# A mixture-of-experts block: six tiles of surplus blocks taken out of the mixed stage and put ahead of the one-expert tiles

## The reference

```python
x = x + jnp.tanh(g_xattn[0]) * _L0_xattn_ref(_layernorm(x, axis=-1), ctx_1024, L0_xattn_W, L0_xattn_b)
x = x + jnp.tanh(g_ffn[0]) * _L0_ffn_ref(_layernorm(x, axis=-1), L0_ffn_expert_sel, L0_ffn_keys, L0_ffn_values)
# _L0_ffn_ref, with xf the 2048 x 256 tokens:
logits = xf @ expert_sel.T
sel = jax.nn.sigmoid(logits)
sel_val, sel_idx = jax.lax.top_k(sel, N_HEADS)          # N_HEADS = 4
gates = gates.at[jnp.arange(N)[:, None], sel_idx].set(sel_val)
h = jnp.einsum('nd,kde->nke', xf, keys)                 # keys 64 x 256 x 128
scores = jax.nn.relu(h) * gates[:, :, None]
out = jnp.einsum('nke,kev->nv', scores, values)         # values 64 x 128 x 256
```

## Time and profile before

| | us |
|---|---|
| median of three runs | 301.71 (300.08 to 302.07) |
| the profiled execution's own time | 301.05 |
| its span, first to last instruction | 299.3 |
| PE / DVE / ACT / POOL busy | 209.5 / 131.7 / 108.9 / 139.1 |

### The profile page before, as it was taken

How to read it: one execution, slowest core, us unless ns; L and a number is a source line. 1 busy time by engine, 2 the same in 40 slices (tenths; PEclk the granted TensorE clock), 3 DMA queues, 4 the chain that set the end, 5 groups by cost and what they waited for, 6 DMA issues and landing times. The chain is left out here.

```text
span 299.3 us, 4532 instructions
## 1 busy us (share of the span) xinstructions
PE 209.5 (70%) x1316; PEld 155.0 (52%) x1316; DVE 131.7 (44%) x496; ACT 108.9 (36%) x307; POOL 139.1 (46%) x156
## 2 busy tenths in 40 slices
PE   7998677549576713398866786939596987613874
PEld 6765545337344401277755575727465665303653
DVE  4478576554754726211221111523251533253674
ACT  3587566637544620033433243413131434200100
POOL 3006745746574766315655665635363655640000
PEclk9999959968755555579999999977686999855998
DMA  5999999999999692377954554533442431129996
GB/s 147 294 307 333 310 353 361 363 344 338 330 288 316 184 320 79 92 206 216 360 183 129 168 148 138 171 93 99 127 134 76 141 103 49 52 69 352 397 414 240
DMA packets 40895, 66.03 MB, mean 221 GB/s; under 512 B 5381, under 2 KB 24603, under 8 KB 40864
## 3 DMA queue, kind: packets, MB, share of 16 engines
q1 hardware_dynamic: 32572, 46.68, 50.0%
q0 software_dynamic: 6624, 16.82, 16.1%
q10 hardware_dynamic: 1668, 2.17, 2.0%
HBM read 38.31 MB, written 28.64 MB: 224 GB/s over the span
## 5 line engine op out<-in xcount | busy, mean ns | idle before, releaser
L525 POOL DMA_INDIRECT y_rows<-rows,by_place x74 | 72.8, 983 | 69.7 <-ACT rows L1042 52.8
L515 POOL DMA_INDIRECT x_slots<-rows,pos_i x64 | 63.5, 992 | 56.4 <-DVE pos_i L1115 33.4
L1293 DVE TENSOR_SCALAR shared<-bank 128x256 f32<-128x256 f32 (+1 forms) x38 | 15.9, 418 | 95.0 <-PE bank L749 42.8
L749 PE MATMUL bank<-xT,keys_sb 128*128 128x128 f32 x256 | 40.1, 299 | 13.3 <-ACT xT L1028 11.8
L1028 ACT COPY xT<-bank 128x512 f32<-128x512 f32 (+1 forms) x38 | 21.9, 577 | 69.1 <-PE bank L743 45.1
L749 PEld LDWEIGHTS bank<-xT,keys_sb 128*128 128x128 f32 x256 | 34.3, 203 | 23.1 <-ACT xT L1028 15.9
L778 PE MATMUL bank<-values_sb,shared 128*128 128x256 f32 x128 | 38.4, 420 | 0.2 <-issue 0.2
L1042 ACT COPY rows<-bank 128x512 f32<-128x512 f32 (+1 forms) x38 | 21.9, 576 | 25.7 <-PE bank L778 12.6
L778 PEld LDWEIGHTS bank<-values_sb,shared 128*128 128x128 f32 x128 | 23.3, 207 | 5.3 <-issue 3.6
L743 PE MATMUL bank<-ident,rows 128*128 128x128 f32 x148 | 23.9, 289 | 0.0
L646 PE MATMUL bank<-values_sb,probsT 120*128 120x320 f32 x32 | 16.7, 611 | 6.6 <-ACT probsT L941 5.0
(11 more groups left out here) (145 smaller groups left out, 323.2 us busy)
## 6 DMA issues: line engine op xcount, KB each, us to landing
x_slots<-values_sb SPq DMA_DIRECT2D x4, 2056.0 KB
rows<-x_slots SPq DMA_DIRECT2D x64, 128.5 KB, 2.1
keys_sb<-y_rows SPq DMA_DIRECT2D x16, 512.0 KB, 5.6
values_sb<-in_L_ffn_values SPq DMA_DIRECT2D x5, 1024.0 KB
xs<-in_x SPq DMA_DIRECT2D x8, 256.0 KB, 7.7
out<-xs ACTq DMA_DIRECT2D x7, 256.0 KB, 5.6
values_sb<-in_L_ffn_values SPq DMA_DIRECT2D x1, 1408.0 KB
rows<-x_slots SPq DMA_DIRECT2D x40, 32.1 KB
```

Of the source, the lines that this page charges most:

```text
L515: pool.indirect_dma_start(x_slots, bass.IndirectOffsetOnAxis(ap=pos_i[:, t * K + k:t * K + k + 1].bitcast(U32), axis=0), rows[:, t % RB * ...
L525: pool.indirect_dma_start(y_rows, bass.IndirectOffsetOnAxis(ap=result_at[:, t:t + 1], axis=0), y_sb[:, t % R, :], None, bounds_check=last_ ...
L749: mm = pe.matmul(pH(place)[:, u * P:(u + 1) * P], keys_sb[:, expert * C + c, :], xgT[:, 2 * ring + u, c * P:(c + 1) * P], start=c == 0, st ...
L1293: dve.tensor_scalar(hidT[:, 2 * ring + part.start:2 * ring + part.stop, :].rearrange("p u n -> p (u n)"), pH(place_of(part, ring))[:, part ...
```

## The change

Six tiles of blocks come first. `MIXED` becomes "eeeeqeeeeeqeee" twice, so 28 tiles with four of blocks; there are 74 tiles and ten tiles of blocks as before.

- *Which blocks.* When tile 12 is counted, DVE notes for each of the first forty experts how many rows it has by then (`early_at`). When all are counted, an expert's blocks of which all rows lie among those are early, the others late. Early ones come first in the table; 24 places (six tiles) are kept for them, and what early blocks are left over goes with the late ones. The table's chain on DVE and PE is therefore gone through twice, first for the early places and then for all.
- *Loads.* SP fetches 24 numbers and loads the 24 blocks when tile 12's scatters have landed, ahead of its wait for the last scatter. A tile's place in the buffer moves by four, so that the first three pairs lie in slots that are free after tiles 11 and 12.
- *Products.* PE turns the three pairs, multiplies them by `hidden_quad` (keys as weights) and `result_quad`, and only then begins the ring of pairs. DVE copies keys for the six tiles (two of them into `keys_early`, a part of the values' buffer that is still free), ACT copies the values. `results_out` of the three pairs waits until tiles 12, 13 and 14 have left the slots that `y_sb` shares.
- *Removed.* The four products at L793 and the wait for the last scatter on PE, and the separate handling of tiles 0 and 1. SP's late loads of values wait for the second early product.

```diff
-    MIXED = "eeqeeqeeeqeeqeeqe" * 2
+    EARLY = 6
+    EARLY_T = 12
+    MIXED = "eeeeqeeeeeqeee" * 2
-    TILES = ALONE + len(MIXED)
-    QUADS = MIXED.count("q")
+    TILES = EARLY + ALONE + len(MIXED)
+    QUADS = EARLY + MIXED.count("q")
...
+        def place_in(t):
+            return (t + Q) % R
...
+            sp.wait_ge(padded, 16 * E // FE)
+            sp.wait_ge(r_early, 1)
+            blocks = rows_at(early_rows[0:1, 0:Q * EARLY], Q * EARLY)
+            for n in range(RB):
+                sp.wait_ge(scattered[n], 16 * K * len(range(n, EARLY_T + 1, RB)))
+            for t in range(EARLY):
+                load_blocks(t, blocks[Q * t:Q * t + Q])
             sp.wait_ge(a_O, T)
-            sp.wait_ge(padded, 16 * E // FE)
             sp.wait_ge(r_first, 1)
             first_rows = rows_at(alone_rows[0:1, 0:2 * R], 2 * R)
...
+            sp.wait_ge(e_H, 2 * 2)
             late_values_in(E - LATE, FREE_VALUES[0])
...
+            for n in range(2):
+                pe.wait_ge(r_unit, 2 * n + 2)
+                pe.matmul(lead_ps, lead[:], unit_of, start=n == 0, stop=False, skip_group_check=True).then_inc(r_block, 1)
+                pe.matmul(expert_ps, expert_col[:], unit_of, start=n == 0, stop=False,
+                          skip_group_check=True).then_inc(r_block, 1)
...
+            def early_hidden(p):
+                pe.wait_ge(e_Tc, 2 * p + 2)
+                for u in range(2):
+                    quad = 2 * p + u
+                    mm = hidden_quad(u, p, At(quad), keys_early[:, quad - 2, :, :] if quad in (2, 3) else None)
+                mm.then_inc(e_H, 2)
+
+            def early_results(p):
+                pe.wait_ge(e_h, 2 * p + 2)
+                after(pe, e_y, 2 * (p - 1))
+                for u in range(2):
+                    mm = result_quad(u, p, p % 2, At(2 * p + u))
+                mm.then_inc(e_Y, 2)
+
             pe.wait_ge(c_Mc, len(units))
             pe.wait_ge(r_table, TABLE)
-            pe.wait_ge(scattered[(T - 1) % RB], 16 * K * len(range((T - 1) % RB, T, RB)))
-            for n in range(4):
-                pe.matmul(bank[:, 7, 0:D], ident[:], values_sb[:, 0, :], start=True, stop=True)
+            slots_T(At(0), 0)
+            slots_T(At(1), 1)
+            early_hidden(0)
+            slots_T(At(2), 2)
+            early_hidden(1)
+            early_results(0)
+            early_hidden(2)
+            early_results(1)
+            early_results(2)
...
+                if s - 3 == EARLY_T:
+                    dve.scalar_tensor_tensor(out=on_diag[:], in0=rank_ps[0:E, :], scalar=float(P - (H - 1)),
+                                             in1=ident[0:E, 0:E], op0=ALU.add, op1=ALU.mult).then_inc(r_landed, 1)
+                    dve.wait_ge(r_landed, 1)
+                    dve.tensor_reduce(early_at[0:ALONE], on_diag[0:ALONE, :], AX.X, ALU.add).then_inc(r_landed, 1)
...
+            own(dve.tensor_scalar(count_i[:, 0:1], end_at[:], over_col[:, 0:1], 0.0, ALU.subtract, ALU.max),
+                dve.tensor_scalar(count_i[:, 1:2], end_at[:], early_at[:, 0:1], 0.0, ALU.subtract, ALU.max))
+            own(dve.tensor_scalar(count_i[:, 2:4], count_i[:, 0:2], H.bit_length() - 1, None, ALU.logical_shift_right))
+            own(dve.tensor_copy(units_f[:], count_i[:, 2:4]))
+            own(dve.tensor_tensor(early_f[:], units_f[:, 0:1], units_f[:, 1:2], ALU.subtract))
...
+            own(dve.tensor_tensor(row_f[:, 0:Q * EARLY], lead_ps[:, 0:Q * EARLY], block_off[:, 0:Q * EARLY], ALU.add))
+            dve.tensor_scalar(early_rows[:], row_f[:, 0:Q * EARLY], 0.0, None, ALU.max).then_inc(r_early, 1)
+            dve.tensor_copy(early_experts[:], expert_ps[:, 0:Q * EARLY]).then_inc(r_early, 1)
...
+            experts = early_block_experts(dve)
+            keys_out(At(0), experts[0])
+            keys_out(At(1), experts[1])
+            keys_out(At(2), experts[2], keys_early[:, 0, :, :])
+            keys_out(At(3), experts[3], keys_early[:, 1, :, :])
+            keep_places(At(0))
+            relu(At(0), 0)
```

More of the change, by code:

```diff
@@ L421, in group_mixed @@
                 each = len(MIXED) // GROUPS
-                for t in range(ALONE + n * each, ALONE + (n + 1) * each):
+                for t in range(EARLY + ALONE + n * each, EARLY + ALONE + (n + 1) * each):
                     if t % 2 == 0:
@@ L733, in _ @@
-            pe.wait_ge(weights_in, 16 * 2 * (E - LATE) // 8)
-            def slots_T(p, ring, part=slice(0, 2)):
-                if part.start == 0 and part.stop == 1:
-                    pe.wait_ge(first_in, 16)
-                else:
-                    after(pe, xg_in[p.mod(PAIRS)], slots_in(p))
-                for u in range(part.start, part.stop):
+            pe.matmul(total_ps, ones_bf[0:E, 0:E], units_bf[:], start=True, stop=True).then_inc(r_end, 1)
+            for n in range(2):
[3 more added lines that the diff above has]
+                          skip_group_check=True).then_inc(r_block, 1)
@@ L742, in slots_T @@
+            pe.wait_ge(weights_in, 16 * 2 * (E - LATE) // 8)
+            def slots_T(p, ring):
+                after(pe, xg_in[p.mod(PAIRS)], slots_in(p))
+                for u in range(2):
                     for c in range(C):
[L743 to L745 removed]
@@ L829, in _ @@
                     quads_turned(n)
-                for part in parts_of(p):
-                    results(p, part)
+                results(p)
             used = rest_used(pe)
@@ L1049, in _ @@
+            for p in range(EARLY_PAIRS, TILES // 2):
                 for n in begun(hidden_by, p):
```

302 lines of the change are left out of this document (168 added, 134 removed).

## The result

The changed kernel takes 326.27 us (median of four runs, 324.16 to 329.47), the kernel before 301.89 beside it (300.08 to 302.81). The ratio is 1.079, 95% interval 1.071 to 1.088: 24 us slower. The profiled execution took 324.16 us, 19.0 more than the 305.2 of the sum.

The account below looks back on a forecast made before the run. No engine is full; chains of waits hold each stage, with a gap at the seam after dispatch to fill. 301.05 + 21.4 (later forty tiles) - 17.3 (mixed tiles) = 305.2 us, range 295.5 to 311.5.

Parts of the forecast that it names:

- The table and the loads: Before the early products: table's first half out at 121.3, loads issued from 123.4, 12.5 us for 24, landing 2.1 after issue.
- I let the clock rise at 138.3: PE's early products: granted clock goes from half to full at 138.3, so product 0 ends at 139.9, product 1 at 144.1.
- the 7.1 us a pair at half: Small products of a pair of early tiles: upper bound 7.1 us at half clock, against 3.6 at full clock.
- the clock's staying at half through product 1: Early products: clock still at half through the second pair's, 3.6 us more; a way into the slower-still case, chance 0.14.
- ACT's copies of values lie there too: Early tiles: ACT's copies of values lie beside the loads, with no time added to the sum.
- 0.8 back: Start of the forty tiles: with all five pairs of buffers loaded, 0.8 us regained, so 22.2 later becomes +21.4.
- Forty tiles left alone: The forty one-expert tiles: pace left unchanged at 1.6 us each, because a full ring stands behind them.
- The mixed tiles: Mixed stage: 28 tiles with one long wait take 51.1 us instead of 68.35, 17.3 less; bounds 12.1 to 21.5.
- The faster one: Rival, 296 us: small products stream at 1.3 us a pair and PE follows the loads; chance 0.24.
- The tie: Rival, 301 us: early tiles as forecast, no long wait in the mixed stage, +21.4 - 21.5; chance 0.22.
- Slower still: Rival, 310.5 us: mixed stage keeps 2.01 us a tile, +21.4 - 12.1; chance 0.14.
- The extra turn: Rival, 313 us: one block more than fits puts a turn into the loop at the end, some 8 us; chance 0.04.

Follow-up runs that it names:

- e1_fill: The changed kernel plus ten unread filling products in PE's two waits for rows ahead of the early products: 319.6 us against 295.6 before, ratio 1.098.
- e11_pieces: The kernel before, with the first product of six of the forty one-expert tiles written as eight products of 32 streamed columns: 265.7 us against 252.4, ratio 1.059.
- e9_mixfill: e1_fill plus 18 unread 256-column products between the small ones of the early tiles: 275.8 us against 252.4 before, ratio 1.094.
- e4_whole: The changed kernel with each early tile multiplied as one expert's tile, the blocks' own products left out: 306.6 us against 295.6 before.
- e5_after_again: The changed kernel run again unaltered in another group: 280.9 us against 252.6 before, ratio 1.122.
- the first group: The follow-up runs on one chip, e1_fill, e2_rows, e3_nofill and e4_whole, where the kernel before took 295.6 us.
- the three variants of the change: e1_fill, e2_rows and e4_whole, each the changed kernel with its early products altered or filled: 319.6, 308.7 and 306.6 us against 295.6 before.
- e3_nofill: The kernel before without its four filling products ahead of the first rows: 298.2 us against 295.6.
- e8_spread: The kernel before, no early tiles, its ten tiles of blocks spread wider (30 one-expert tiles first, then 44 mixed): ratio 0.999.
- e2_rows: The changed kernel with early tiles multiplied in the mixed stage's form, blocks as weights and keys streamed at 128 columns: 308.7 us, ratio 1.050.

## Why the prediction was wrong, point by point

**The table and the loads: right, in part by luck.** First half out at 120.4 (121.3 forecast), first 32-row load at 124.16 (123.4), 24 issues in 13.5 us (12.5). The table was 0.9 early, and between the fetch's end at 122.4 and the first load passed 1.8 us for which my sum had 0.3; the two partly cancel. The 2.1 us to landing I took from the row of 128-row loads; the earlier trace rows gives none for the small ones. The first product began at 135.91 (134.4): 1.5 us of the miss.

**The failed step is the clock's rise: "I let the clock rise at 138.3".** It rose only after 166. I let it rise some 5 us after PE took up work, because it had in before, from 125.28. But before was at work with products of 128 and 256 columns, and after with a stream of 32-column ones. e1_fill shows this form losing a clock that was up, e11_pieces shows it amid a busy stretch, e9_mixfill shows the same products keeping it when wider ones stand between, and e4_whole shows it rising with the same idleness ahead once the form is gone. The price that I had read from the earlier trace rows, 0.111 us a record, was right at full clock, and the 7.1 us a pair at half that I named as a bound is what all three pairs paid (6.7, 6.8 and 7.0). I had this outcome for the products up to the second pair's ("the clock's staying at half through product 1", 3.6 more) and not for the whole stage.

What it cost, against the forecast's own terms: products 20.5 us in place of 12.7, so 7.8; results 6.0 in place of 3.3, 2.7; the turn of pair 2, 0.3. That is 10.8 of the 14.3 us by which the forty tiles started later than forecast. The late start of the first product makes 1.5, and 2.1 is the wait that I had hidden in "ACT's copies of values lie there too": two buffers for six tiles of values, so ACT can copy the next ones only when the results before them are out. The sum of these is 14.4.

**"0.8 back" at the first scatter: wrong in sign.** The wait for values and the low clock stand right before the forty tiles, whose first products run at half: 1.6 more and not 0.8 less, a difference of 2.4.

**"Forty tiles left alone": 5.7 more, and not by the change.** e5_after_again has them at 51.1. On the chip of the first group the three variants of the change have them at 64.8 to 65.7 and e3_nofill, which is before but for its filling, at 65.7: same chip, same time, with the change and without. A steady pace of some 1.3 us a tile is interrupted by waits. Before has them in its forty tiles as well, and I had looked for them only in the mixed stage. POOL's scatters come late there at 143.49, 153.51, 163.46, 173.46 and 183.53, ten microseconds apart and all in tiles of one expert. The waits view of before, from 133 to 197 (us in all, times, longest):
```profile
ACT xT L1028 <- remote: 15.0, 4, 3.8
```
and the same view of e8_spread over both long stages, 118 to 215, in which "remote", a release that the trace can't place, doesn't occur:
```profile
ACT xT L1033 <- PE bank L748: 31.4, 33, 3.2
```

**The mixed tiles: 20.1 less (17.3 forecast, 12.1 to 21.5), for a wrong reason.** I hung the long waits on tiles of blocks. Where there are none, moving six tiles out saves what six tiles cost: 68 tiles take 88.4 us from the first scatter to the last in e5_after_again, 74 take 96.2 in e8_spread, 7.8 less or 1.3 each. The 20.1 is this, plus the longer waits in before's mixed stage. The first group's chip has such waits too: 34 mixed tiles took 64.1 us in e3_nofill and 28 took 47.2 to 50.2 in the three variants, 14 to 17 less. On the quiet chip, with e8_spread in before's place, the bill is plain: first turn of the forty tiles 35.1 later (149.51 against 114.38), 2.8 more to their first scatter, 7.8 saved: 30.1, and the spans differ by 30.3.

The deviations add up: 14.3 + 2.4 + 5.7 - 2.8 and 0.5 less in the combining are 19.1 of the 19.0 us.

**The rivals.** The faster one hung on 1.3 us a pair, which only the mixed stage's form has (e2_rows). The tie's term for the mixed stage, 21.5 less, came near the 20.1 measured; its late start was the forecast's and failed with it. "Slower still" named the right mechanism, the clock's staying down, at a third of its size (3.6 of 10.8 us); its other term, a mixed stage that keeps 2.01 a tile, didn't come. The extra turn didn't either: 74 scatters and 40 block loads ran. Also with the good form, split loads and split copies, no version beat before. The changed kernel turns its first early rows at 130.71, where before turned its first ordinary ones at 128.83; in e5_after_again and e8_spread it is 114.84 and 114.38. So the early loads bring PE nothing sooner, and there was no gap to fill, only work moved to a place where it overlaps with less. In e5_after_again the first 32-row load is issued at 99.21 and PE still waits for it 15.6 us, with the DMA engines full (share 1.00 from 105 to 110). And where POOL sets the pace, six tiles out of the stages give back six scatters, 7.7 us, while the shortest early stage took 15.1.

**Open:** what the long waits are and why only some chips show them, and whether tiles of blocks set them off there.

## What to carry to other kernels

Ask of each new stretch of TensorE work not only whether it keeps the engine busy but which products it streams: here 32-column products behind full 128-column weights cost as much as 128-column ones and, where they stood alone, ran at half clock, they and what followed until wider work was back. Writing the blocks as weights with the wide operand streamed avoided it, and so did wider work in between. Before a gap is filled, see in the trace whether the first new piece could land earlier than the old first piece did. And before tiles are moved out of a stage, ask what one tile costs there on its slowest engine: here one POOL scatter, 1.28 us.

## What the runs showed of the hardware that I had not expected

- The granted clock fell from 1.00 to 0.50 with PE 100% busy, in e1_fill and e11_pieces, and came back when the 128-column products with keys did.
- With full weights, records that stream 32 columns and records that stream 128 stand equally far apart, 0.111 us at full clock (e11_pieces, e4_whole).
- Unread work made a kernel faster: 28 products more, ratio 1.094 in place of 1.122, over runs of before that agree to 0.2 us though on another chip; the early stage is 4.6 us shorter.
- The same program took 14% less time in another group of runs (280.9 us in place of 326.3), with forty tiles in 51.1 us in place of 69.4, while its early stage agreed to 0.1 us. A pace per tile read from one execution isn't the kernel's own.
